# The last of nine taps leaves GpSimd: its product is reduced by VectorE in PSUM, and every engine's order is written anew

## The reference, cut to what matters

```python
for oy in (0.0, 1.0):
    for ox in (0.0, 1.0):
        yy, xx = (y0 + oy, x0 + ox)
        wgt = (1.0 - jnp.abs(ys - yy)) * (1.0 - jnp.abs(xs - xx))
        ...
        out = out + jnp.where(valid, wgt, 0.0)[..., None] * g
...
return jnp.einsum('npkgc,npkg->npgc', out, mk).reshape(B, H, W, G * Cg)
...
d = _dcn_core(v, off, mask) @ op_w.T
z = d @ cv2_w.T
```

## Time and profile before

| | us |
|---|---|
| median of 3 runs (lowest, highest) | 1060.81 (1060.80, 1062.05) |
| the profiled execution's own time | 1062.49 |
| its span, from the first to the last instruction | 1060.6 |
| mean granted TensorE clock | 0.675 |
| busy PE / DVE / ACT / POOL | 651.9 / 570.5 / 319.2 / 466.6 |
| taps and convolution, from the first unit's product to the last sum's end | 54.7 to 479.7 |
| first experts, attention, second experts end near | 678, 885, 1060 |

### The profile page before, as it was taken

The page is one execution under the profiler, slowest core; times in us unless marked ns, Lnnn a source line. Parts: engine busy times, 40 slices in busy tenths (PEclk is TensorE's granted clock), DMA queues, the critical chain, the costliest instruction groups (busy, mean ns, idle before and its releaser), DMA issues.

```text
span 1060.6 us, 10454 instructions
## 1 busy us (share of the span) xinstructions
PE 651.9 (61%) x3032; PEld 474.3 (45%) x3032; DVE 570.5 (54%) x1032; ACT 319.2 (30%) x520; POOL 466.6 (44%) x364
## 2 busy tenths in 40 slices
PE   1585776675866665542688888384857573656611
PEld 0354555553645454431455666263646452433300
DVE  3359687868767677853466655343434434333311
ACT  1434444124445241000355555230211111322300
POOL 0068688878694968984000000304363521000055
PEclk9677768567768685555799999755555555655555
DMA  6245354415454334200555554000000002433311
GB/s 240 67 112 128 87 135 117 120 43 125 124 129 113 86 74 110 60 0 15 173 160 163 163 157 133 17 1 10 11 16 10 15 6 56 114 84 92 91 30 37
DMA packets 79927, 90.75 MB, mean 86 GB/s; under 512 B 54782, under 2 KB 60158, under 8 KB 79870
## 3 DMA queue, kind: packets, MB, share of 16 engines
q1 hardware_dynamic: 75328, 84.68, 29.6%
q0 software_dynamic: 4096, 4.20, 1.7%
q10 hardware_dynamic: 446, 1.20, 0.3%
HBM read 37.67 MB, written 14.61 MB: 49 GB/s over the span
## 4 chain that ended last, share of the span: by engine, by line
PE 27%; issue 22%; POOL 16%; DVE 15%; ACT 8%; SPq 7%; DMA 3%; POOLq 0%; DVEq 0%; ACTq 0%
POOL sb_acc L1334 7%; POOL sb_yg L1365 4%; SPq L406 3%; POOL xs L1346 3%; PE ps_pa L474 3%; DVE sb_prod L1071 3%; PE ps_t L509 2%; PE ps_c L467 2%; PE ps_t L576 2%; PE ps_pb L594 2%; DVE sb_hats L1148 2%; PE ps_c L495 2%; ACT sb_hats L848 2%; SPq L402 1%; SPq L403 1%
## 5 line engine op out<-in xcount | busy, mean ns | idle before, releaser
L1334 POOL TENSOR_TENSOR sb_acc<-sb_acc,sb_prod 128x1024 f32<-128x1024 f32 x128 | 301.7, 2383 | 53.5 <-DVE sb_prod L1071 53.0
L1365 POOL DMA_INDIRECT sb_yg<-ys,sb_jdx x64 | 60.9, 952 | 326.8 <-DMA ys<-sb_yt 307.9
L509 PE MATMUL ps_t<-sb_vbd,sb_hx 128*128 128x256 f32 x576 | 139.3, 388 | 76.1 <-DVE sb_prod L1071 68.4
L1071 DVE TENSOR_TENSOR sb_prod<-ps_t,sb_hy 128x1024 f32<-128x1024 f32 x128 | 153.6, 1215 | 60.1 <-PE ps_t L509 38.7
L509 PEld LDWEIGHTS ps_t<-sb_vbd,sb_hx 128*128 128x128 f32 x576 | 109.0, 266 | 107.8 <-DVE sb_prod L1071 78.3
L1346 POOL DMA_INDIRECT xs<-sb_xr,sb_idx x64 | 64.1, 1002 | 23.4 <-issue 15.3
L1201 DVE TENSOR_TENSOR sb_hid<-ps_t,sb_hid 114x512 f32<-114x512 f32 x69 | 46.5, 686 | 44.6 <-ACT sb_hid L869 40.9
L495 PE MATMUL ps_c<-sb_dwT,sb_omx 128*128 128x256 f32 x144 | 53.4, 527 | 22.5 <-DVE sb_hats L1057 18.9
L869 ACT ACTIVATE sb_hid<-ps_t 114x512 f32<-114x512 f32 x69 | 41.2, 599 | 46.0 <-PE ps_t L577 46.0
L495 PEld LDWEIGHTS ps_c<-sb_dwT,sb_omx 128*128 128x128 f32 x144 | 35.5, 263 | 31.8 <-issue 26.0
L1371 POOL TENSOR_TENSOR sb_rs<-sb_mv,sb_epst 128x2 f32<-128x2 f32 x32 | 6.3, 197 | 91.5 <-DVE sb_mv L1007 91.4
(11 more groups left out here) (253 smaller groups left out, 1409.8 us busy)
## 6 DMA issues: line engine op xcount, KB each, us to landing
sb_hx<-sb_hats SPq DMA_DIRECT2D x384, 96.0 KB, 2.2
sb_acc<-in_wcat SPq DMA_DIRECT2D x16, 876.0 KB, 4.5
xs<-sb_x3t SPq DMA_DIRECT2D x16, 512.0 KB, 4.7
sb_yrep<-in_wcat SPq DMA_DIRECT2D x7, 876.0 KB, 4.6
sb_nt<-xs SPq DMA_DIRECT2D x64, 64.0 KB, 2.0
ys<-sb_yt SPq DMA_DIRECT2D x55, 64.0 KB, 1.9
sb_acc<-in_ucat SPq DMA_DIRECT2D x22, 160.0 KB, 2.3
sb_xt<-xs SPq DMA_DIRECT2D x46, 64.0 KB, 2.0
```

Source lines behind the costliest of these rows:

```text
L509: last = mm(tb[u % 2][:, j * 256:(j + 1) * 256], hx[q % 3][:, j, o:o + P], vbd[n % 2][:, j * 256:(j + 1) * 256], start=True, stop=True)
L1071: v.tensor_tensor(o.rearrange("p (g c q) -> p g c q", g=G, q=H), tb[u % 2][:, :].rearrange("p (g c q) -> p g c q", g=G, q=H), w, ALU.mult) ...
L1334: g.tensor_tensor(acc[n % 2][:, t, :], acc[n % 2][:, t, :], prod[a % 3][:, :], ALU.add).then_inc(s_pool_acc, 1)
L1365: g.indirect_dma_start(out=yg[b][:, t, z, :], out_offset=None, in_=ys[0:NJT[m] * TILE, :], in_offset=bass.IndirectOffsetOnAxis(ap=jdx[m][: ...
```

## The change

The units of the last tap (k = 8) no longer go to GpSimd. VectorE writes their product back into the PSUM tile that it read, waits for its own product, and sums it over the 16 rows into a new tile `dlast`; only that sum frees the PSUM tile. TensorE then joins `dsum` and `dlast` with four products by the identity, two accumulating for each half, instead of two transposes. GpSimd does 14 adds to an image.

```diff
-ADDS = UNITS - TT
+ADDS = UNITS - 2 * TT
...
+        dlast = sb("dlast", [P, TT, C])
...
             def sampled(n):
                 pe.wait_ge(s_dve_dr, n + 1)
+                pe.wait_ge(s_dve_p, UNITS * (n + 1))
                 if n:
                     pe.wait_ge(s_dve_rk[0], n)
-                to_channels(pb, dsum).then_inc(s_pe_dt, 1)
+                for t in range(TT):
+                    mm(pb[0:C, t * P:(t + 1) * P], dsum[:, t, :], ident[:, :], start=True, stop=False)
+                    last = mm(pb[0:C, t * P:(t + 1) * P], dlast[:, t, :], ident[:, :], start=False, stop=True)
+                last.then_inc(s_pe_dt, 1)
...
                     o = acc[n % 2][:, t, :]
+                elif k == K - 1:
+                    o = tb[u % 2][:, :]
                 else:
...
-                                w, ALU.mult).then_inc(s_dve_p, 1)
+                                w, ALU.mult).then_inc(s_dve_last if k == K - 1 else s_dve_p, 1)
+                if k == K - 1:
+                    dve.wait_ge(s_dve_last, TT * n + t + 1)
+                    if n:
+                        dve.wait_ge(s_pe_dt, n)
+                    v.tensor_reduce(dlast[:, t, :], o.rearrange("p (c r) -> p c r", r=H), AX, ALU.add).then_inc(s_dve_p, 1)
...
             def tap(n, k, t):
-                if k == 0:
+                if k in (0, K - 1):
                     return
```

More of the change, by code:

```diff
@@ L39 @@
     "sp": """
-        zzzzzzzzaa aaaapaaaaz zaapzzpaaa zzpaaazzpp ppaaaaaaxx xxxdxdxdxd xdxdxdxdxd xdxdxdxdxd xdxdxdxdxd xddddxxxxx xxxddddxxx
+        zzzzzzzzaa aaaapaaazz paaazzpaaa zzpaaazzpp ppaaaaaaxx xxxdxdxdxd xdxdxdxdxd xdxdxdxdxd xdxdxdxdxd xddddxxxxx xxxddddxxx
         xddddxxxxd dddxddddeo eoeoeo
@@ L43 @@
     "pe": """
-        aaaaaaaaaa aaaaattttt atattaaata aaaattatta tttaattttt ttataptaaa paaaaaptta tttapttpta apttttatat ttaaataaaa aptaptttta
-        pttattptpt tpttttttpp ttapttapap ttaaataaaa aptatttata atttpptpat attaaapaaa aapttatpat taatttttaa taaataaaaa ttaptptapt
-        ptpaatttpt tttttaataa ataaaaatta ttpaptptat tptpttpttt tttttttttt ppttptttpp ttptttttpp ppppxxuudd uxuduudddx dududduxud
+        aaaaaaaaaa aaaaattttt atattaaata aaaattatta tttaatttaa ptaaapaaaa apttatttap ttptaapttt tatataaata aaaattapap ttpttptpat
+        attptttttt aataaataaa aattapaptt pttptpatat tpttttttaa taaataaaaa ttapapttpt tptpatattp ttttttaata aataaaaatt apapttpttp
+        tpatattptt ttttaataaa taaaaattap apttpttptp atttpttttt tttttttptp ttptttpptt ptttttttpp ppppxxuudd uxuduudddx dududduxud
         udduxddudu dduxududdu xddududdux ududduxddu dudduxudud duxddududd uxududduxd dududduxud udduxddudu dduxududdu xddududdux
-        ududduxddu dudduxudud duxddududd uxududdudu duddduddee eeeoeooeeo eoeoeoeooo ooeeeeeeee eooeoeooeo ooooooeeee eeeeeooeoe
-        ooeooooooo eeeeeeeeeo oeoeooeooo ooooxuxddu xdduxdduxd uxuxuddddd ddxuxduxux udddddddxu xduxuxuddd ddddxuddeo eoeoeo
+        ududduxddu dudduxudud duxddududd uxududdudu duddduddee eeoeoeooee oeooeoeoeo ooeeeeeeoo eeoeooeoeo oeooooeeee eeooeeoeoo
+        eoeooeoooo eeeeeeooee oeooeoeooe ooooxuxddu xdduxdduxd uxuxuddddd ddxuxduxux udddddddxu xduxuxuddd ddddxuddeo eoeoeo
         """,
     "act": """
-        aaaaaaaaaa aaaaaaaaaa papapaaaap paaaaapapa aapapppppa papaaaaaaa pppaaapapa aaaaaaaaap papaappaaa aaapapaapp papppppppp
+        aaaaaaaaaa aaaaaaaaaa papapaaaap paaaaaapap apappaaaaa apapapappa aaaaapapap appaaaaaap apapappaaa aaapapapap papppppppp
         ppxxuuxxuu xxduuduuxx uudxxuuduu xxuudxxuud uuxxuudxxu uduuxxuudx xuuduuxxuu dxxuuduuxx uudxxuuduu xxuudxxuud uuxxuudxxu
-        uduuxxuudx xuuduuxxuu dxxuuxuduu deeeeeoooe ooeeoooeee eeeoeeoooo oooeeeeeeo eeoooooooe eeeeeoeeoo oooooxxuxx duxxduxxdu
+        uduuxxuudx xuuduuxxuu dxxuuxuduu deeeeoeoeo oooeeooeee eeoeooooee oooeeeeeoe ooooeeoooe eeeeoeoooo eeoooxxuxx duxxduxxdu
         xxduxxuxxu dddxxuxxdu xxuxxudddx xuxxduxxux xudddxxxud eoeoeoeo
@@ L57 @@
     "dve": """
[L58 to L62, removed]
+        aaaaaaaaat taatattttt tttaaaatat atatttaapa tttptaptta aaptatatap ttpaapttat ttttpataaa taptaptpta tptttptptt aattattttp
+        ataaatapta ptptatpttt ptpttaatta ttttpataaa taptaptpta tptttptptt aattattttp ataaatapta ptptatpttt ptpttaatta ttttpataaa
+        taptaptpta tptttptptt attttttttp tttptpttpt pttptptttt tttppppppp xxxuuxxuux xduuuduxxu udxxuuudux xuudxxuuud uxxuudxxuu
+        uduxxuudxx uuuduxxuud xxuuuduxxu udxxuuudux xuudxxuuud uxxuudxxuu uduxxuudxx uuuduxxuud xxxuxuuudu deeeoooeee eooeeeooeo
+        eooeoeoooe eeeeoooeee ooeeeooeoe eoooooeoee eeoooeeeoo eeeooeoeeo ooooeoeeee oooeeeooee eooeoeeooo oooxxxuxxd uxxduxxuxx
         uxxuxxdudd dxxuxxuxxu xxdudddxxu xxuxxuxxdu dddxxxdxud eoeoeoeo
@@ L65 @@
     "pool": """
-        ttaatttttt ttttttttta tttttttttp tttttptpta ttttttttts tttttptttp tptttttttt tapttttptt ptttsttttt satptttttp ptstttattt
-        tttttttptt ptpttttatt tttttttstt ptttptpttt tttttttttt tttptttptp ttttttttss pppseoeeoo eeeeeoeeoo ooooeeeeeo eeooooooee
-        eeeoeeoooo ooeeeeoooo eoeoeoeo
+        ttaatttttt tttttttttt ttatpttttt ptptattttt tttttspttt ptpttttatt ttttttttsp tttptptttt attttttttt tsptttptpt tttatttttt
+        ttttsptttp tpttttattt tttttttspt ttptpttttt ttttttttts ttptttptpt ttttttttts pppseoeeoo eeoeeoeooe eoooeeeeoe ooeoeoooee
+        eeoeooeoeo ooeeeeoooo eoeoeoeo
         """,
@@ L298, in build @@
         s_hx = [sem(f"s_hx{s}") for s in range(3)]
-        s_pe_t, s_dve_p, s_pool_acc, s_dve_dr, s_pe_dt, s_act_dt, s_pe_z, s_act_z, s_dve_x1, s_pe_x1t, s_act_x1 = map(sem, (
-            "s_pe_t", "s_dve_p", "s_pool_acc", "s_dve_dr", "s_pe_dt", "s_act_dt", "s_pe_z", "s_act_z", "s_dve_x1", "s_pe_x1t",
+        s_pe_t, s_dve_p, s_dve_last, s_pool_acc, s_dve_dr, s_pe_dt, s_act_dt, s_pe_z, s_act_z, s_dve_x1, s_pe_x1t, s_act_x1 = map(sem, (
+            "s_pe_t", "s_dve_p", "s_dve_last", "s_pool_acc", "s_dve_dr", "s_pe_dt", "s_act_dt", "s_pe_z", "s_act_z", "s_dve_x1", "s_pe_x1t",
             "s_act_x1"))
```

## The result

The changed kernel takes 1094.59 us (median of 4 runs, 1094.0 to 1095.53), the kernel before 1061.43 beside it (1060.8 to 1063.06): a ratio of 1.0309, 95% interval 1.0293 to 1.0324. The profiled execution has a span of 1093.7 us, 33.1 longer than before.

The account below looks back on a forecast made before the run. It took GpSimd's adds to bind one part of each image and VectorE's preparation the other. Taps +9.9 and attention +13.4 made +23.3: 1085.8 us in the profile's terms, 1084 for the median, range 1064 to 1097.

Parts of the forecast that it names:

- The period: Taps, from one image's depthwise product to the next's: four legs sum to 56.9 us against 52.7, +16.8 over four periods.
- The first three legs: Within a taps period: 22 us to product (n+1,1,0), 22.2 of GpSimd's adds, 1.8 to the norm's end.
- the second leg: GpSimd binds: eight adds 18.6, 1.5 for the norm, 1.6 waiting for `rank`, 0.5 hits and picks; 22.2 us.
- The last leg: From the norm through transposition, 1x1 product, ScalarE and depthwise to the next unit (n+1,8,0): 10.9 us.
- The stage: The whole taps stage, its periods with start, last part and the chain after the last add: +9.9 us.
- The start: The first two images of the taps: the depthwise of image 3 comes at 154.8 against 157.33, -2.5 us.
- rival 4: Taps: VectorE's norm goes before the add, the period loses 1.5 us, 6 over four: 1078; chance 0.12.
- The attention: GpSimd's new order makes a pair's period 53.3 us against 46.7, +6.6 twice; with first and last pair +13.4.
- 1: Taps: adds resume within some 6 us of the last tap's, all 37.1 us come out: 1038; chance 0.08.
- 2: The attention alone loses; the taps' period stays 52.7 us: +13, 1074; chance 0.14.
- 3: The taps alone lose; the attention's period is bound by a chain both orders share: +9.9, 1071; chance 0.10.
- 5: The taps gain what the attention loses, -13 in the taps: within 0.2% of now; chance 0.03.

Follow-up runs that it names:

- e3: The edit's code as in the changed kernel, with all five strings in the order of the kernel before: 1070.59 us, ratio 1.0080.
- e9: As e3, but VectorE's sum of the last tap's product takes only the first of the 16 rows: 1060.36 us, ratio 0.9974.
- e10: The changed kernel, with GpSimd's inverse root for images 4 and 6 put before the scatter of images 3 and 5: 1094.81 us, ratio 1.0285.
- e1: The changed kernel, with the attention's part of the five strings put back as before the change: 1074.61 us, ratio 1.0123.
- e2: The kernel before, with only the attention's part of the five strings in the changed order: 1078.71 us, ratio 1.0149.
- e7: The edit, attention's order as before, a fourth order of the taps found by walking the strings, zeros 8 to 15 later: 1028.24 us, ratio 0.9674.
- e8: The kernel before without the edit (16 adds), its taps in an order searched for as in e7, zeros 8 to 15 later: 1025.37 us, ratio 0.9653.
- e5: The edit, attention's order as before, a third order of the taps with late steps behind the next image's first adds: 1065.22 us, ratio 1.0020.
- e11: The changed kernel, attention's order within a pair as before the change, GpSimd's order between pairs as changed: 1093.47 us, ratio 1.0297.
- e12: As e11, with GpSimd's root for images 4 and 6 before the scatter of 3 and 5 as in e10: 1084.38 us, ratio 1.0201.

## Why the prediction was right, and where it was not

**The period (56.9 forecast, 57.8 measured).** The walk along the strings held leg by leg. From the end of unit (2,8,0) at 214.79 the product (3,1,0) ends at 236.97, 22.2 later (forecast 22); the eight adds end at 259.4 (22.4, forecast 22.2); the norm of image 5 ends at 261.3 (1.8, forecast 1.8). The first three legs were right within 0.2 us, and so was the sum in PSUM (1.21 forecast, 1.224 measured). Inside the second leg the wait for `rank` was shorter than forecast (0.77 against 1.6), and a wait for a product (0.91), which had no term, made up for it. The last leg, norm to the next unit (n+1,8,0), was mis-sized: 273.07 - 261.28 = 11.8 against 10.9, because the depthwise product took 5.21 at a granted clock of 0.53 and not the 4.34 of the earlier trace rows at 0.64. The 52.7 that the forecast started from is a mean of four periods of 42 to 70 us; after the change they are all alike, 56.6 to 58.5.

**The stage (+9.9 forecast, +11.0 measured).** The start gained 5.2 (157.33 to 152.15; forecast 2.5), the four periods lost 20.5 (forecast 16.8), the last part gained 2.9 and the tail 1.4, as forecast. The start came out 2.7 better and the periods 3.7 worse than forecast, so that the nearness of the sum is in part luck. The sentence that the 16 adds lay in the part that GpSimd binds does not hold: in e3 some 31 of their 37 us turn up as waits, and in e9 they are worth 5.7. The sum had no term for them, so the number did not suffer by it.

**The norm's lock (rival 4).** The norm lost: it took 2.70 and ended 0.3 after the add beside it, and the next add came 1.49 late, the 1.5 of the forecast. It is so in all four images. The Trainium skill (SBUF — State Buffer, section on who interferes with whom) says that whichever issues first holds the shared port for its whole length and the other waits. That the norm waited for the whole add, the trace shows; which of the two issued first, it does not settle, for their starts lie within 0.1 us of each other (236.97 and 237.05 here), the norm's first in two images and the add's in the other two.

**The attention (+13.4 forecast, +16.5 measured).** The rise of the period was forecast as 6.6 and measured as 7.6 to 7.7, the first pair's as 1.4 and 1.5; the last pair, forecast to gain 1.2, gained 0.35. The legs that the forecast lists for GpSimd, 22.7 by its sum, add up to 23.0, and the trace has 23.2 (788.89 to 812.06); from the queries to the scatter it has 31.2 against 30.6. The size was nearly right and the cause incomplete: the walk followed the even images and blamed the scatter ahead of the root. e10 removes just that and gains nothing, since the odd images' chain was as long. That nothing of the taps enters, e1 and e2 show.

**What was left out.** 4.4 us at the end of the first experts had no term. The same products of the same tiles ran there at a granted clock of 0.50 (680 to 690 us) where the kernel before had 0.99 (669 to 675.2). Until those products the changed kernel trails by 10.8 (676.15 against 665.32), about what the taps cost, and at the gather by 15.4. Over five runs, the time from the root of image 7 to the first gather goes with the granted clock of its last 20 us: 190.7 at 0.93 before the change, 192.9 and 193.2 at 0.81 in e9 and e3, 195.1 at 0.62 in the changed kernel and in e1. With 1.2 in the second experts this is over half of the 9.7 by which the profiled forecast of 1085.8 fell short of the execution's 1095.5 (1093.7 and 1.9); the attention makes 3.1 of the rest and the taps 1.1.

**The rivals.** 1 fell: no add ran for 21 us and not 6, and the string had the boundary's work ahead, as its condition said. Its idea, that half of that work can go behind the first adds, is right in another order (e7), though it isn't the freed adds that pay there: e8, with all 16, is as fast. 2, 3 and 5 each left out a loss that was there. The low end of the range, 1064, does not come out of the terms named for it, which give 1060 with the gains at both ends of the stage and 1067 without them; nothing hangs on it here.

## What to carry to other kernels

An engine that has the most work and idles once a round need not be the bound: count where the work taken off lies, in the stretch where the others wait for it or in the one where it waits itself. Price an order by walking it engine by engine with the rows' durations; and when one step seems to hold a loop, look for a second chain of the same length before naming it. An edit's worth can be hidden by the order that comes with it, so measure the edit in the old order too: here the edit alone cost 0.8% (e3), with the orders that came with it 3.1%, and with another order of the taps it ran 3.3% under the kernel before (e7).

## What the runs showed that was not expected

**A waiting VectorE instruction can lose to an add that starts after it.** `values` of VectorE and the adds beside it, in e7:

```profile
257.52 5.70 DVE L1037 SCALAR_TENSOR_TENSOR sb_vbd<-sb_vh,sb_wide,sb_vm 128x1024 fp32r<-128x1024 f32 x1
```

```profile
250.53 11.60 POOL L1346 TENSOR_TENSOR sb_acc<-sb_acc,sb_prod 128x1024 f32<-128x1024 f32 x5
```

Five adds ran back to back there. The fourth was running when `values` came (it ended at 259.84), and the fifth, from 259.81 to 262.13, went ahead of it although `values` had waited for 2.3 us: it ended 1.1 after that add, about its own time. In e5 it took 3.45 behind one add, and the next add beside it took 3.34. So in these runs the stretch without adds is where such an instruction was cheap.

**The granted clock moved where the order of the work did not.** In the changed kernel it fell during the last two tiles of the first experts, near 678.3, with TensorE busy 2.51 of the 4 us from 672 to 676 at the upper level and no pause above 1.7 us before it fell; before the change the same products kept the upper level to their end. In e1 it rose for a while in the first pair of the attention (0.64 from 706.4 to 730.4, against 0.50 in the changed kernel), and that pair's first scatter came 28.9 us after its queries, where the changed kernel took 32.1, though the order differs too. In e11 the clock did the same and the scatter came after 28.8; in e12, whose steps up to the end of that pair are the same as e11's on all five engines, it did not (0.50), and the scatter came after 31.7. What decides this was not tried.
